# A post-norm decoder on one core: the first self-attention group split in two halves of two batches

## What is computed

```python
# first sub-layer, per batch: 16 heads of width 8
q, k, v = x @ Wq + bq, x @ Wk + bk, x @ Wv + bv
own     = softmax(q k^T / sqrt(8)) v                   # per head, 128x128 scores
own     = own @ Wo + bo
rq      = own @ Wrq + brq                              # attends two past states of 256 tokens
past    = sum over 2 pasts of softmax(rq rk^T / sqrt(8)) rv
gate    = sigmoid([own, past] @ Wg + bg)
x       = layernorm(x + mix of own and past by gate)
```

## Time and profile before

| | |
|---|---|
| median of three executions | 608.4 us |
| the profiled execution, its own time | 603.48 us |
| its span, first to last instruction | 601.7 us |
| mean granted TensorE clock | 0.976 |
| busy: PE, DVE, ACT, POOL | 516.8, 454.3, 332.0, 214.8 us |
| engine that holds most of the chain that ended last | PE, 58% |
| first maximum-scores matmul of batch 0 | at 19.16 us |

### The profile page before, as it was taken

How to read it: one execution, slowest core, us unless ns; L and a number is a source line. 1 busy time by engine, 2 the same in 40 slices (tenths; PEclk the granted TensorE clock), 3 DMA queues, 4 the chain that set the end, 5 groups by cost and what they waited for, 6 DMA issues and landing times.

```text
span 601.7 us, 14032 instructions
## 1 busy us (share of the span) xinstructions
PE 516.8 (86%) x5226; PEld 281.4 (47%) x5226; DVE 454.3 (75%) x1017; ACT 332.0 (55%) x572; POOL 214.8 (36%) x333
## 2 busy tenths in 40 slices
PE   2588888899999999999998787778989976979784
PEld 0255554233333333333335565543443566879673
DVE  4367777889989898988955887837766657967686
ACT  2066665477887878778766665630111163427761
POOL 7113211701112411332332614334234284775452
PEclk9989999699999999999999999999999998979999
DMA  5445420130002203032012223053864500001001
GB/s 149 120 112 143 118 77 2 47 102 2 20 19 56 71 2 93 4 94 72 19 35 72 68 68 83 4 182 104 279 217 165 200 0 2 2 17 37 2 22 49
DMA packets 46558, 44.04 MB, mean 73 GB/s; under 512 B 6998, under 2 KB 37462, under 8 KB 46486
## 3 DMA queue, kind: packets, MB, share of 16 engines
q1 hardware_dynamic: 44476, 42.01, 23.7%
q10 hardware_dynamic: 2016, 1.15, 0.8%
HBM read 25.18 MB, written 1.18 MB: 44 GB/s over the span
## 4 chain that ended last, share of the span: by engine, by line
PE 58%; DVE 13%; ACT 9%; issue 7%; DMA 6%; POOL 4%; SPq 2%; ACTq 1%; DVEq 0%; POOLq 0%
PE banks L1180 11%; PE banks L1160 7%; PE banks L554 5%; ACT probs L709 5%; PE banks L1095 5%; PE banks L1776 5%; PE banks L462 4%; PE banks L537 3%; DMA past_mem<-gates 2%; DVE rec_negmax L1409 2%; PE banks L1191 2%; PE banks L512 1%; DVE shared L1890 1%; DVE negmax L853 1%; PE banks L1139 1%
## 5 line engine op out<-in xcount | busy, mean ns | idle before, releaser
L1409 DVE TENSOR_REDUCE rec_negmax<-banks 128x2 bf16<-128x512 f32 x256 | 165.8, 687 | 24.0 <-PE banks L1095 21.8
L1302 ACT ACTIVATE probs<-banks 128x1024 f32<-128x1024 f32 x128 | 131.1, 1025 | 48.5 <-PE banks L1160 47.3
L853 DVE TENSOR_REDUCE negmax<-banks 128x8 bf16<-128x1024 f32 x64 | 78.2, 1221 | 45.1 <-PE banks L512 45.0
L1095 PE MATMUL banks<-shared 62*128 62x512 bf16 x256 | 97.0, 397 | 4.3 <-DVE rec_negmax L1409 3.7
L1160 PE MATMUL banks<-shared 64*128 64x256 bf16 x512 | 97.8, 278 | 0.2 <-DMA shared<-rec_neg_T 0.2
L1180 PE MATMUL banks<-probs,past_mem 128*32 128x256 f32 x1024 | 82.7, 395 | 1.3 <-ACT o_T L1309 1.3
L709 ACT ACTIVATE probs<-banks 128x1024 f32<-128x1024 f32 x64 | 65.5, 1024 | 32.8 <-PE banks L537 32.7
L1776 PE MATMUL banks<-shared,w_r 128*128 128x512 f32 x128 | 60.8, 613 | 6.5 <-DVE shared L1890 6.5
L1160 PEld LDWEIGHTS banks<-shared 64*128 64x128 bf16 x512 | 30.1, 94 | 69.8 <-issue 64.7
L554 PE MATMUL banks<-probs,shared 128*32 128x128 f32 x1024 | 42.0, 282 | 21.0 <-ACT probs L709 20.8
L1890 DVE TENSOR_TENSOR shared<-past_mem,out_T 128x512 f32<-128x512 f32 x64 | 42.9, 693 | 14.7 <-DMA past_mem<-gates 14.4
(11 more groups left out here) (248 smaller groups left out, 968.8 us busy)
## 6 DMA issues: line engine op xcount, KB each, us to landing
past_mem<-gates SPq DMA_DIRECT2D x64, 256.0 KB, 4.9
shared<-qk_parts SPq DMA_DIRECT2D x90, 128.0 KB, 2.5
shared<-past_mem SPq DMA_DIRECT2D x30, 128.0 KB, 2.7
xk_T<-in_x_T SPq DMA_DIRECT2D x4, 256.0 KB, 3.2
shared<-rec_neg_T SPq DMA_DIRECT2D x64, 2.0 KB
xk_T<-in_ctx_T SPq DMA_DIRECT2D x4, 256.0 KB, 3.7
Y<-in_x SPq DMA_DIRECT2D x4, 256.0 KB, 3.9
w_r<-in_w_r SPq DMA_DIRECT2D x4, 256.0 KB, 3.4
```

The lines of the kernel that those rows point to most:

```text
L853: nc.vector.tensor_reduce(c.negmax[:, i % 2, :].rearrange("p (r j) -> p r j", r=2)[:, :, 4 * half:4 * half + 4], c.max_pair.rearrange("p ( ...
L1095: self.nc.tensor.matmul(c.max_banks[r], c.QT[64 * r:64 * r + 62, g % 2, j, off:off + P], c.rKT[64 * r:64 * r + 62, j, :], start=True, stop ...
L1302: nc.scalar.activation(c.probs[:, i % 4, :], c.score_pairs[i % 2], ACT.Exp, scale=HEAD_SCALE)\
L1409: self.nc.vector.tensor_reduce(out, c.max_banks[r].rearrange("p (a t) -> p a t", a=NP_PAST), AX_X, ALU.max, negate=True).then_inc(s["rec_m ...
```

## The change

The first group of four batches is handled as two halves of two batches (256 columns). A new name prefix, `first_`, stands for the first half, while `self_` group 0 is now the second half. x of group 0 comes in two loads, `first_x` (batches 0, 1) and `self_x0` (batches 2, 3), and the second of them is issued after w_qk and b_qk. PE projects q and k of the first half, then those of the second, into four banks of their own. ACT and DVE split the first half (both `high`s, both `middle`s), ACT issues the k spread of the first half, and only then splits the second half. SP issues the q spread of the first half, the constant rows, then the q and the k spread of the second half, then q of group 1, x of group 2, and k of group 1. `load_past`, `load_out` and `load_prep` move from steps 0, 1, 2 to 4 of SP's loop to its steps 4, 5 and 9. `max_scores` waits for the first half's spreads in slot 0, and for the second half's in slot 2. `window(0)` and `window(1)` move: on PE from after `project_v(0)`, `project_v(1)` to just behind the first maximum scores of slots 1 and 2; on ACT from before `copy_neg`, `rows` to behind them; on DVE they stay.

```diff
+def first_half(name):
+    return slice(0, PAIR) if name.startswith("first_") else slice(PAIR, 2 * PAIR)
...
 def split_bank(c, name, g):
+    if g == 0 and name in ("first_q_", "first_k_", "self_q_", "self_k_"):
+        bank = {"first_q_": 6, "first_k_": 4, "self_q_": 7, "self_k_": 5}[name]
+        return c.banks[:, bank, 0:PAIR]
...
-    return c.score_banks[0] if g == 0 and name == "self_k_" else c.proj_bank
+    return c.proj_bank
...
@@ PE, max_scores
+            if i or cross:
+                pe.wait_ge(*s.after(ph + "qt%d" % gp, 96 * (g // 2 + 1)))
+                pe.wait_ge(*s.after(ph + "kt%d" % gp, 96 * (g // 2 + 1)))
+            else:
+                pe.wait_ge(*s.after("first_qt", 96))
+                pe.wait_ge(*s.after("first_kt", 96))
+        if half == 0 and i == 2 and not cross:
+            pe.wait_ge(*s.after("self_qt0", 96))
+            pe.wait_ge(*s.after("self_kt0", 96))
@@ PE, begin and slot
         pe.wait_ge(*s.after("load_first", c.n_load_first * 16))
-        project_q(0)
-        project_k(0)
+        for name, landed in (("first_", "first_x"), ("self_", "self_x0")):
+            pe.wait_ge(*s.after(landed, 16))
+            for n, which in enumerate(("q_", "k_")):
+                project(name + which, 0, c.w_qk[:, n, :], c.xk_T[:, 0, first_half(name)])
...
             max_scores(t, 0)
...
+        if not cross and t in (1, 2):
+            window(t - 1)
...
-        window(t)
+        if cross or t >= 2:
+            window(t)
@@ ACT, begin
-        high_of("q", 0, 0)
-        middle_act(c, act, "self_q_", 0, c.qk_parts[:, 0], c.left[:, 0, :])
-        high_of("k", 1, 0)
-        middle_act(c, act, "self_k_", 0, c.qk_parts[:, 1], c.left[:, 1, :])
-        act.wait_ge(*s.after("set_zero", 2))
-        spread_rows(c, act, "self_k_", 0, c.KT[:, 0], c.qk_parts[:, 1], K_ORDER, "self_kt0")
+        for name in ("first_", "self_"):
+            over = first_half(name)
+            for n, which in enumerate(("q_", "k_")):
+                high(c, act, name + which, 0, bias[:, n:n + 1], c.qk_parts[:, n, :, over])
+            for n, which in enumerate(("q_", "k_")):
+                middle_act(c, act, name + which, 0, c.qk_parts[:, n, :, over], c.left[:, n, over])
+            if name == "first_":
+                act.wait_ge(*s.after("set_zero", 2))
+                spread_rows(c, act, "first_k_", 0, c.KT[:, 0, :, over], c.qk_parts[:, 1, :, over], K_ORDER, "first_kt")
@@ ACT, slot
-        if t:
+        if t and (cross or t > 2):
             window(t - 1)
         if 0 <= t - 1 < B and not (cross and t - 1 < 2):
             copy_neg(t - 1)
             rows(t - 1)
+        if not cross and t in (1, 2):
+            window(t - 1)
@@ DVE, begin
-        rest_of("q", 0, 0)
-        low_dve(c, dve, "self_q_", 0, c.qk_parts[:, 0], c.left[:, 0, :])
-        rest_of("k", 1, 0)
-        low_dve(c, dve, "self_k_", 0, c.qk_parts[:, 1], c.left[:, 1, :])
+        for name in ("first_", "self_"):
+            over = first_half(name)
+            for n, which in enumerate(("q_", "k_")):
+                rest(c, dve, name + which, 0, bias[:, n:n + 1], c.qk_parts[:, n, :, over], c.left[:, n, over])
+            for n, which in enumerate(("q_", "k_")):
+                low_dve(c, dve, name + which, 0, c.qk_parts[:, n, :, over], c.left[:, n, over])
@@ SP
-        load(0)
-        others("first")
+        for name, landed in (("first_", "first_x"), ("self_", "self_x0")):
+            b = first_half(name).start // P
+            sp.dma_start(c.xk_T[:, 0, first_half(name)].rearrange("p (b t) -> p b t", b=2),
+                         x_T[b:b + 2].rearrange("b p t -> p b t")).then_inc(s[landed], 16)
+            if name == "first_":
+                others("first")
         load(1)
         sp.wait_ge(*s.after("set_zero", 2))
-        queries(0)
+        over = first_half("first_")
+        spread_rows(c, sp, "first_q_", 0, c.QT[:, 0, :, over], c.qk_parts[:, 0, :, over], Q_ORDER, "first_qt")
         others("rows")
+        over = first_half("self_")
+        spread_rows(c, sp, "self_q_", 0, c.QT[:, 0, :, over], c.qk_parts[:, 0, :, over], Q_ORDER, "self_qt0")
+        spread_rows(c, sp, "self_k_", 0, c.KT[:, 0, :, over], c.qk_parts[:, 1, :, over], K_ORDER, "self_kt0")
+        queries(1)
+        load(2)
+        keys(1)
-    for t in range(4 if cross else 0, B + 2):
+    for t in range(4, B + 2):
...
-                elif step == 0:
+                elif step == 4:
                     load_all(sp, load_past, "load_past")
-                elif step == 1:
+                elif step == 5:
                     load_all(sp, load_out, "load_out")
-                elif step in (2, 3):
-                    load_all(sp, load_prep[3 * (step - 2):3 * (step - 1)], "load_prep")
-                elif step == 4:
-                    load_all(sp, load_prep[6:], "load_prep")
+                elif step == 9:
+                    load_all(sp, load_prep, "load_prep")
```

More of the change, by code:

```diff
@@ L310, in declare @@
     s.own("set_", "memset zero zero_rest bias warm")
+    s.own("first_", "x")
     s.own("past_", "proj hi rest mid lo kt v_proj v")
@@ L313, in declare @@
     s.own("cross_", "x_norm keep x_turned x_t out_prod out stats")
-    s.own("one_", "kv0 kv1")
+    s.share([("first_", "qt=96 kt=96"), ("one_", "kv0 kv1")])
     s.own("rq_", "proj hi rest mid lo")
@@ L323, in declare @@
     for which in ("q_", "k_"):
-        s.share([(ph + which, "proj=4 hi=4 rest=4 mid=4 lo=4") for ph in ("self_", "cross_")])
+        s.share([("first_" + which, "proj=1 hi=1 rest=1 mid=1 lo=1")]
+                + [(ph + which, "proj=4 hi=4 rest=4 mid=4 lo=4") for ph in ("self_", "cross_")])
     s.own("ln1_", "aggr ln")
@@ L502, in max_scores @@
         if half == 0 and i % 4 == 0:
-            pe.wait_ge(*s.after(ph + "qt%d" % gp, 96 * (g // 2 + 1)))
-            pe.wait_ge(*s.after(ph + "kt%d" % gp, 96 * (g // 2 + 1)))
+            if i or cross:
[7 more added lines that the diff above has]
+            pe.wait_ge(*s.after("self_kt0", 96))
         if half or i:
@@ L529, in scores @@
                 pe.wait_ge(*s.after("load_rows", 16 * (1 + NP_PAST)))
+                pe.wait_ge(*s.after("self_k_rest", 1))
         if half or i:
@@ L1045, in attention_sp @@
             others(t)
-        if t == 0 and not cross:
-            load(2)
         if t == 4:
```

## The result

The changed kernel takes 603.16 us (median of 20 executions) against 605.64 for the kernel before (median of 20 beside it): ratio 0.9955, 95% interval [0.9934, 0.9976], some 2.7 us of 605 faster. Forecast were 4.1. The mean of the four, weighted by their intervals, is 0.9956 [0.9942, 0.9970]. The four spread more than their intervals allow for (0.9908 and 0.9977 lie 0.007 apart), so this interval is rather too narrow.

What follows compares the result with a forecast made beforehand. PE was taken to bound the kernel (58% of the last chain), but a chain of waits its first 19 us. Start 4.7, plus 0.4, minus 1.0 gave 4.1 us off the 608.4 median: 604.3, range 600.8 to 608.0.

Steps and rivals of the forecast that it cites:

- Part 1: First loads: less of x ahead of b_qk on SP lets PE start 0.3 us earlier, bounds 0 and 0.45.
- Part 2: From PE's start to the first k issue on ACT: halved projection and split save 2.2 us, bounds 1.5 and 2.9.
- Part 3: First k spread: six issues stay 3.98 us, last landing falls from 4.90 to 2.7; saves 2.2, bounds 0 and 2.6.
- Part 4: Slot 1, window(0) moved behind the maximum scores: net gain 0.4 us, bounds 0 and 1.
- Part 5: Slot 2, group 1's k projected between the two exponentials: costs 1.0 us, between 0.2 and 1.85 by PE's clock level.
- The covers: Spreads land before they are wanted: by 0.7 to 2.5 us in slot 2, by 2 in slot 4.
- B: Rival: PE at the faster level from slot 2 on and stays; gain 6.1 us, total 602.3; chance 0.20.
- E: Rival: slower, as PE stays at 1.2 GHz in slots 2 to 5; total 612.9; chance 0.08.
- C: Rival: the last landing stays near 4.9 us for either half; total 606.0 to 606.5; chance 0.11.
- D: Rival: first scores 4 us earlier, but a later step, likely SP's queue, takes it back; total 608; chance 0.09.

Runs made afterwards that it cites:

- e1: The changed kernel run again with no edit; ratio to the kernel before 0.9977 [0.9946, 1.0007].
- e7: The changed kernel run again with no edit, for a third profile; ratio to the kernel before 0.9908 [0.9870, 0.9945].
- e10: The changed kernel run again with no edit, for a fourth profile; ratio to the kernel before 0.9969 [0.9938, 1.0001].
- e8: e4 with the low part's k spread issued by SP instead of ACT, and b_qk loaded first on ACT's queue; ratio to the kernel before 0.9931.
- e3: The kernel before with only the past, output and preparation loads moved behind group 1's spreads, no halves; ratio 0.9983 [0.9949, 1.0016].
- e11: e4 with twelve unread projections added on PE behind the first ones, two more in each of slots 0 and 1; ratio to the kernel before 0.9925.
- e12: e8 with nine unread projections added on PE and two more in slots 0 and 1; ratio to the kernel before 0.9923.
- e5: The changed kernel with load_past, x of group 2, load_out and load_prep back at their old places; ratio to the kernel before 1.0000.
- e2: The kernel before run again with no edit; ratio to itself 0.9989 [0.9955, 1.0022].
- e9: The kernel before run again with no edit, for a third profile; ratio to itself 1.0015 [0.9984, 1.0046].
- e4: The changed kernel with the projections of slots 0 and 1 at their old places on PE and ACT; ratio to the kernel before 0.9962.

## Why the forecast came out as it did

**Part 1**, the loads: 0.3 forecast, PE began at 4.45 in the first profile, at 4.50 in e1, 4.23 in e7 and 4.56 in e10, so 0.42 to 0.75 earlier than 4.98, three times of four over the upper bound of 0.45. Mean against mean (4.98, 4.92 and 4.83 in the profiles of before) it is 0.47, just at that bound. The bound counted x's packets alone; in e8, with b_qk on the other queue, PE began at 3.63.

**Part 2**, projection and split: 4.45 to 7.65 is 3.2 us, 3.5 to 3.6 forecast; 0.47 and 0.48 for the steps against 0.48 and 0.42. It saved 2.6.

**Part 3**, issues and landing: the six issues took 4.18, not 3.98. From their end to the first scores passed 3.14. The last landing took 3.6, 2.8, 3.5 and 2.7, not 2.7 each time. The forecast sum was right by errors that cancel, which is luck: the first scores at 14.97, 14.18, 14.57 and 14.14 in four profiles, mean 14.5, the forecast's number. The cause was put down too simply, as e3 shows: the loads make 1.3 of the 2.2 us.

**Part 4**, window(0): 10.3 us from first scores to first exponential, against 10.87 before; 10.4 forecast.

**Part 5**, window(1): between 2.5 and 4.2 forecast, by PE's level; 3.47, 3.33, 3.15, 2.41 measured, as the projection took 2.08, 1.63, 1.45 and 1.13. So the level differs from execution to execution, and the middle (3.35) was a good value to take; the mean is 3.09.

**The covers** held: no wait in slot 2 or 4. In slot 2 the last spread had landed 2.3 to 3.5 us before it was wanted (0.7 to 2.5 forecast). In slot 4 it was 0.2, 0.6, 1.4 and 0.6 us in the four profiles, not 2: the slots before it ran faster than in the first profile of before, so that the scores came at 33.3 to 35.0 and not at 37.4. This thin cover is what e11 and e12 ran into. The list missed one wait, `high_of` of group 1 for the q spreads, which e5 exposed.

**The total**: 4.1 forecast, 4.6 in the traces up to 320 us, 2.7 (1.8 to 3.5) timed. The direction and the mechanism of the start came out, the size in the total came out a third smaller. The step that carried least is the sentence that a start that is earlier should end the program earlier by about that amount. It held for the first half in all profiles. Behind it the spread between executions of one program is as large as the difference, and I named clock effects only for the start (rivals B and E), not for the rest.

That the measured 603.16 lies only 1.1 from the forecast 604.3 is luck. The forecast took its gain off a median of three executions, 608.4; the median of 20 is 605.64, and 4.1 off that gives 601.5. The chance of 0.62 stood on a gain of over 0.5%; it came out at 0.45%, in the part that had 0.29.

**The rivals**: C fell (no landing near 4.9), and its 606.0 should read 605.8, since 604.3 and 1.5 are that. E fell too, as PE was at the faster level from 29 us on at the latest. D fell as it was put, with no gain in the total; a part of the lead is lost behind 320 us, but not where D looked for it, at SP's queue around slots 4 to 10: at 320 us each lead is within 0.5 us of that at 57. B's condition was met in e10, where PE rose at 22 us and stayed up to 104: its lead at 57 us is 6.2, B's number 6.1. But 1.2 of these 6.1 is the slow stretch around 34 us of one profile of before. e2 and e9 don't have it and stand 0.9 and 1.2 ahead, so that this part is no gain of the change.

## What to carry to other kernels

When the first wait of a kernel is a chain of projection, split, copy and landing, halving the first piece shortens projection, split and landing, but not the issues (six took 4.18 us after 3.98), and the full gain needs a queue that holds nothing between the halves. List each wait on the buffers that are reused, not only the data's way to its reader. Count issues per queue and even them out: with one issue and one small load on the other queue the first scores came 2.2 us earlier, of which 1.4 were left at 57 us. Work out again how much later waits are covered once the start is earlier. A lead of 1% in a trace should be followed to several places and over several profiles before it is called gained or lost.

## What the runs showed of the hardware

**The granted clock column can be blank about the start.** In the first profile of before it reads 1.00 up to 30 us, where the projection's 1.92 and the scores' 0.60 are of the 1.2 GHz level; the earlier trace rows have the same. In the changed kernel's it reads 0.50 there, with scores of the same 0.61. The same stretch in the changed kernel, then in the kernel before:

```profile
12.00:20.00 8.00, 3.11 (x28) 2.07 (x29) 4.65 (x8) 1.76 (x5) 0.00 (x0) 0.50 0.39 100
```

```profile
12.00:20.00 8.00, 0.61 (x8) 0.37 (x8) 0.24 (x2) 0.00 (x0) 0.00 (x0) 1.00 0.96 238
```

So the mean clock of a whole span leaves the start out in the one and counts it in the other. Durations of a known instruction tell the level.

**Executions of one program differ by several us, and the clock goes with it.** Twelve executions of e11 ran from 593.2 to 602.0 us, the fastest at a mean clock of 0.983, the others at 0.964 to 0.971. The four profiles of the changed kernel span 598.1 to 603.9 us: the clock falls at four places in each, and stays low for longer, or falls again, in some. The Trainium skill (TensorE: Matmul & The Clock Gate, section What's actually happening) holds that the monitor's window runs free and does not begin anew with the kernel; falls that differ between executions of the same instructions agree with that, but don't prove it.

**Work that nobody reads can pay.** 16 projections more on PE made the kernel faster, since they kept the clock up: slots 0 and 1 took 3.2 us less (e11 against e4), and e11 and e12 ran 3.3 us shorter than the changed kernel on the same chip (e12 has the even queues as well).

**An issue costs the same at half the size.** The line of the spreads in the changed kernel (duration ns min/median/max) has 0.60 and 0.63 us for 64 KB on SP and ACT, as before for 128 KB (0.60 and 0.64); the landing's least fell from 2.4 to 2.0, and the median over the first group's twelve spreads from 2.9 to 2.1 (the 2.4 of the earlier trace rows has later groups in it). The changed kernel up to 20 us:

```profile
L453 SPq DMA_DIRECT2D shared<-qk_parts x18: 590/598/635, 6.3 to 19.4; - x18
L453 ACTq DMA_DIRECT2D shared<-qk_parts x6: 618/633/855, 7.6 to 11.2; - x6
```
